# Attention's transfers on SP: each group waits for the landing of an earlier one, and k's two parts move as one run

## The chip, the cores and the metric

The kernel runs on one core of a Trainium2 chip. Its time is the device time of one execution in microseconds (us); three executions before the change took 1617.93, 1617.93 and 1624.52 us, so the median is 1617.93 us. Engines are named as in the profile: PE (TensorE matmul, PEld its weight load), DVE (VectorE), ACT (ScalarE), POOL (GpSimd), SP (SyncE, which here does nothing but issue transfers; the profile writes SPq). 16 DMA engines carry out the transfers that SP, ACT and POOL issue.

## The reference

One gated block on x of shape (16, 128, 1024) with a context of the same shape:

```python
x = x + tanh(g_xattn) * attention(layernorm(x), ctx)   # 8 heads of 16 channels, window of 16 positions
x = x + tanh(g_ffn)   * ffn(layernorm(x))              # weights int4-like integers, groups of 128

q = Wq x + bq ; k = Wk cond + bk ; v = Wv cond + bv    # pointwise over 128 channels
k, v are padded with 8 zeros on the left and 7 on the right of the 1024 positions
dots[b,h,t,w] = sum_d q[b,h,d,t] * k[b,h,d,t+w] / 4 ;  attn = softmax over w (16 places)
out = Wo (sum_w attn * v[.., t+w]) + bo
ffn = (silu(x Wgate) * (x Wup)) Wdown                  # 1024 -> 3584 -> 1024
```

k, q, v and the probabilities are held as a high and a low fp16 part whose sum carries the fp32 value; the products of both parts are summed.

## The kernel before

The span has two stages. The first 418 us or so are attention over the 16 batches, the rest is the feed-forward part, 14 passes over its hidden columns. The change touches attention only.

**One round of attention** (loop over `b`, 16 rounds) handles batch b in four steps (`s` = 0 to 3). A step's scores are 64 small matmuls (L1100) into two banks, the softmax runs on DVE (L896, L900), ACT (L679) and POOL (L546, L548), PE transposes the probabilities (L1111), ACT copies them (L684) and PE mixes them with v (64 matmuls, L1131). The projections of the batch after, b + 1, are set between those steps by `tasks_of`: k in step 0 (PE L1062, ACT L668 writes the high part, DVE L932 the low part), v in step 1 (PE L1058, ACT L662, DVE L928), q in step 2, and the output product of batch b - 1 in step 3. Every engine runs its own program in order; a semaphore wait at an instruction holds all that stands behind it on that engine.

**SP's part of a round** is a fixed list of issues, in this order: `keep_row(b - 2)` stores a finished batch to device memory (L423, 512 KB); `move_k(b + 1)` copies the two halves of k from `k_hl` into the staggered buffer `km` in 8 transfers of 64 KB, 16 partitions each (L394), SBUF to SBUF; `load_ctx(b + 2)` loads the next context (L382, 512 KB); `place_v(b + 1)` copies v from `vn_hl` into `vt` in two copies of 6 transfers each (L406, L408, L410), with 40, 8, 48, 48, 40 and 8 partitions (the last 8 and the first are the spill over the edge); `load_x(b + 2)` loads x (L376, 512 KB). In the kernel before, SP waits in this list only for engines: for k's low part (the wait in `move_k`, DVE L932), for v's low part, for buffers that the engines have read. It never waits for a transfer to land, except for `row_kept` of four batches ago and before the first weights of the second stage.

**Who waits for SP's transfers:** PE's scores of batch b + 1 for all 8 moves of k; PE's first mix of batch b + 1 for all 12 moves of v; PE's projections of k and v for the context; DVE's moments for x. Two waits go the other way round a buffer: ACT L668 may write k_hl only when the last batch's 8 moves have landed (`k_moved`), and ACT L662 may write `vn_hl` only when the last batch's 12 moves have landed (`v_placed`).

Of the kernel before, what the change touches and what calls it, by code (L numbers as in the profile page):

```python
# [4 lines left out]
def flamingo_layer(nc, x_in, ctx_in, g_xattn, g_ffn, WqT, bq, WkT, bk, WvT, bv, WoT, bo,  # L5
# [62 lines left out]
    with ctx:  # L68
# [26 lines left out]
        k_hl = sb("k_hl", [P, 2, T], fp16, att)  # L95
# [6 lines left out]
        km.append(sb("km1", [P, 2, HG, T + WIN], fp16, att))  # L102
# [40 lines left out]
        V_MOVES = 16 * 2 * (VW + 2)  # L143
# [5 lines left out]
        def slot_of(j):  # L149
# [28 lines left out]
            sem("zeroed"), sem("consts_made"), sem("masks_made"), sem("gates_ready"))  # L178
        km_zeroed = [sem("km0_zeroed"), sem("km1_zeroed")]
        bias_turned, bias_summed, bias_ready = sem("bias_turned"), sem("bias_summed"), sem("bias_ready")  # L180
        pad_hi, pad_lo, pad_placed, ones_placed = sem("pad_hi"), sem("pad_lo"), sem("pad_placed"), sem("ones_placed")
        x_loaded = [sem("even_x_loaded"), sem("odd_x_loaded")]
        ctx_loaded, k_moved, v_placed, row_kept = sem("ctx_loaded"), sem("k_moved"), sem("v_placed"), sem("row_kept")
# [185 lines left out]
        def _(sp):  # L369
            def load_x(b):  # L370
                if b >= 4:
                    sp.wait_ge(row_kept, 16 * (b - 3))
# [3 lines left out]
                sp.dma_start(rows[b % 4][:, :], x_in[b]).then_inc(x_loaded[b % 2], 16)  # L376

            def load_ctx(b):
# [3 lines left out]
                sp.dma_start(ct[:, :], ctx_in[b]).then_inc(ctx_loaded, 16)  # L382

            def move_k(b, halves=(0, 1)):

                sp.wait_ge(emptied_proj, low_done("k", b, 1))
                if b < 2:
# [8 lines left out]
            def place_v(b):  # L396
# [5 lines left out]
                for d in (0, KW):  # L402
                    for jj in range(VW):
                        lo, slot = QB * jj - PAD, jj * NV
                        a, z = max(lo, 0), min(lo + KW, P)
                        sp.dma_start(to[d + a - lo:d + z - lo, slot:slot + NV], vn_hl[a:z]).then_inc(v_placed, 16)  # L406
                        if lo < 0:
                            sp.dma_start(to[d:d - lo, slot + 1:slot + NV], vn_hl[P + lo:P, 0:NV - 1]).then_inc(v_placed, 16)  # L408
                        if lo + KW > P:
                            sp.dma_start(to[d + P - lo:d + KW, slot:slot + NV - 1], vn_hl[0:lo + KW - P, 1:NV])\  # L410
                              .then_inc(v_placed, 16)
# [891 lines left out]
```

## Time and profile before

| | |
|---|---|
| runs shown, median of 3 | 1617.93 us |
| profiled execution: its own time | 1623.17 us |
| profiled execution: span of the core | 1621.4 us |
| PE busy, of the span | 95% |
| DVE busy, of the span | 90% |
| granted TensorE clock, mean | 0.985 |
| SP's transfers (q1), share of 16 DMA engines, 60 to 380 us | 66.6% |

The profiled execution is 5.2 us above the median of the runs shown, and within what those runs span. A busy share is a mean over both stages. In attention the engines are less full than in the feed-forward part, and how SP spends a round is only seen in its list of issues in order of time: the start of an issue is where SP's wait ended, and its duration is what SP needs to hand it over, not what the transfer takes.

### The profile page before, as it was taken

The page shows a single profiled execution, that of the slowest core. Times are in us where ns is not written, and L with a number is a line of the kernel's source. Part 1 is how long each engine was busy: PE and PEld are TensorE (multiplying, and loading weights), DVE is VectorE, ACT ScalarE, POOL GpSimd, SP SyncE. Part 2 cuts the span into 40 slices and gives each one's busy share as a digit, 9 for nine tenths or more (in the row PEclk, how much of TensorE's full clock was granted, in tenths as well). Part 3 has the DMA queues.
Part 4 walks back from the last instruction along what each step waited for, and adds up shares of the span by engine and source line. Part 5 has one row for each costly group of instructions (what it writes and reads, how often), then busy time and mean ns, then how long its engine had stood idle before and what let it go on. Part 6 is the DMA issues. An engine that isn't in the chain of part 4 may idle for free.

```text
span 1621.4 us, 38499 instructions
## 1 busy us (share of the span) xinstructions
PE 1534.6 (95%) x15590; PEld 789.4 (49%) x15590; DVE 1454.5 (90%) x1425; ACT 1057.2 (65%) x1207; POOL 1262.2 (78%) x948
## 2 busy tenths in 40 slices
PE   6888898988799999999999999999999999999996
PEld 4565566665444444444444444444444444444444
DVE  4688788887798999999999999999999999999997
ACT  3677777877566666666666666666666666666652
POOL 3677677778455988888888888888888888888865
PEclk7899999999899999999999999999999999999999
DMA  4676766775353767666667676666666676666569
GB/s 126 171 155 140 172 145 148 173 159 138 118 143 98 152 154 155 152 151 152 147 153 156 156 155 151 149 153 152 152 155 156 144 156 156 153 152 151 116 182 324
DMA packets 192267, 250.16 MB, mean 154 GB/s; under 512 B 14446, under 2 KB 138030, under 8 KB 192074
## 3 DMA queue, kind: packets, MB, share of 16 engines
q1 hardware_dynamic: 167994, 164.26, 36.8%
q0 software_dynamic: 22752, 82.85, 29.1%
q8 instruction: 124, 2.03, 0.5%
q10 hardware_dynamic: 1344, 0.59, 0.2%
q14 instruction: 53, 0.43, 0.1%
HBM read 113.92 MB, written 16.78 MB: 81 GB/s over the span
## 4 chain that ended last, share of the span: by engine, by line
PE 86%; ACT 5%; issue 4%; POOL 2%; DVE 1%; DMA 1%; SPq 1%; ACTq 0%; DVEq 0%; POOLq 0%
PE bank L1193 69%; PE bank L1111 3%; PE bank L1100 2%; ACT pT L684 2%; PE bank L1066 2%; PE bank L1131 2%; PE bank L1073 2%; PE bank L1062 2%; PE bank L1058 1%; ACT vn_hl L662 1%; POOL oacc L628 1%; PE bank L1078 1%; PE bank L1090 1%; ACT pr L679 1%; ACT xn L692 1%
## 5 line engine op out<-in xcount | busy, mean ns | idle before, releaser
L988 DVE SCALAR_TENSOR_TENSOR acc<-bank,scale,acc 128x1024 f32<-128x1024 f32 x784 | 969.5, 1279 | 51.7 <-PE bank L1193 14.9
L1193 PE MATMUL bank<-xT,w_int 128*128 128x512 f16 x3584 | 847.8, 379 | 6.3 <-DVE xT L940 2.0
L628 POOL TENSOR_TENSOR oacc<-oacc,d_part 128x1024 f32<-128x1024 f32 x219 | 536.3, 2454 | 54.5 <-ACT d_part L832 49.0
L1193 PEld LDWEIGHTS bank<-xT,w_int 128*128 128x128 f16 x3584 | 350.3, 98 | 431.4 <-DVE xT L940 3.3
L832 ACT ACTIVATE d_part<-bank,scale 128x1024 f32<-128x1024 f32 x219 | 244.1, 1115 | 200.8 <-PE bank L1193 196.9
L1193 PE MATMUL bank<-h_hi,d_int 128*128 128x512 f16 x896 | 339.6, 379 | 2.1 <-ACT d_part L832 1.8
L1193 PE MATMUL bank<-h_lo,d_int 128*128 128x512 f16 x896 | 339.6, 379 | 0.0
L832 ACT ACTIVATE d_more<-bank,scale 128x1024 f32<-128x1024 f32 x158 | 176.2, 1115 | 154.4 <-PE bank L1193 154.4
L630 POOL DMA_DIRECT2D oacc<-d_more x158 | 149.9, 949 | 114.0 <-ACT d_more L832 107.8
L564 POOL TENSOR_TENSOR raw_z<-raw_w,raw_z 128x512 int32<-128x512 int32 x168 | 225.6, 1343 | 16.5 <-DMA raw_z<-in_L_ffn_gate_z_dram 8.3
L684 ACT ACTIVATE pT<-bank 96x1024 f16<-96x1024 f16 x128 | 130.2, 1017 | 38.3 <-PE bank L1111 37.9
L618 POOL TENSOR_TENSOR h_lo<-acc,h_hi 128x1024 f16<-128x1024 f32 x56 | 129.5, 2312 | 22.7 <-ACT h_hi L814 22.7
L1193 PEld LDWEIGHTS bank<-h_hi,d_int 128*128 128x128 f16 x896 | 87.7, 98 | 107.9 <-ACT d_part L832 2.0
L1193 PEld LDWEIGHTS bank<-h_lo,d_int 128*128 128x128 f16 x896 | 87.7, 98 | 104.3
L801 ACT ACTIVATE acc<-bank,scale 128x1024 f32<-128x1024 f32 x112 | 118.9, 1111 | 11.9 <-PE bank L1193 11.9
L546 POOL CAST p_hl<-pr 128x768 f16<-128x768 f32 x64 | 52.8, 824 | 73.8 <-ACT pr L679 68.4
L548 POOL TENSOR_TENSOR p_hl<-pr,p_hl 128x768 f16<-128x768 f32 x64 | 105.5, 1648 | 5.3
L1111 PE MATMUL bank<-ident,p_hl 128*128 128x128 f16 x1024 | 82.4, 224 | 8.4 <-issue 6.5
L896 DVE TENSOR_REDUCE rmax<-bank 128x16 f32<-128x768 f32 x64 | 61.1, 954 | 31.7 <-PE bank L1100 31.1
L995 DVE SCALAR_TENSOR_TENSOR acc<-acc 128x1024 f32<-128x1024 f32 x56 | 80.8, 1443 | 0.5
L806 ACT ACTIVATE acc<-acc 128x1024 f32<-128x1024 f32 x56 | 59.2, 1057 | 31.5 <-DVE acc L988 31.5
L1111 PEld LDWEIGHTS bank<-ident,p_hl 128*128 128x128 f16 x1024 | 64.8, 100 | 30.2 <-issue 23.9
(85 smaller groups left out, 1438.5 us busy)
## 6 DMA issues: line engine op xcount, KB each, us to landing
oacc<-d_more POOLq DMA_DIRECT2D x158, 512.0 KB, 5.0
raw_w<-in_L_ffn_gate_w_dram SPq DMA_DIRECT2D x56, 256.0 KB, 3.4
raw_z<-in_L_ffn_gate_z_dram SPq DMA_DIRECT2D x56, 256.0 KB, 4.2
raw_w<-in_L_ffn_up_w_dram SPq DMA_DIRECT2D x56, 256.0 KB, 3.4
raw_z<-in_L_ffn_up_z_dram SPq DMA_DIRECT2D x56, 256.0 KB, 4.0
raw_w<-in_L_ffn_down_w_dram SPq DMA_DIRECT2D x56, 256.0 KB, 3.1
raw_z<-in_L_ffn_down_z_dram SPq DMA_DIRECT2D x56, 256.0 KB, 3.7
vt<-vn_hl SPq DMA_DIRECT2D x64, 198.0 KB
```

The source lines that it names most:

```text
L548: nc.gpsimd.tensor_tensor(lo, src, hi, ALU.subtract).then_inc(p_lo, 1)
L564: nc.gpsimd.tensor_tensor(raw_z[:, slot], raw_w[:, slot], raw_z[:, slot], ALU.subtract)\
L618: nc.gpsimd.tensor_tensor(h_lo[:, q % 2, :], acc[:, q % 2, 0, :], h_hi[:, q % 2, :], ALU.subtract)\
L628: nc.gpsimd.tensor_tensor(into, into, d_part[:, (n - 1) % 2, :], ALU.add).then_inc(d_added, 1)
L630: nc.gpsimd.dma_start(into, d_more[:, (n - 1) % 2, :], accum_op=ALU.add).then_inc(landed(n)[0], 16)
L684: nc.scalar.activation(pT[0:2 * KW, n % 2, hg, :], turned[0:2 * KW, :], ACT.Copy).then_inc(pT_ready, 1)
L801: nc.scalar.activation(acc[:, q % 2, m, :], pair[u % 4][:, :, :].rearrange("p h r -> p (h r)"), ACT.Copy, scale=scale[:, par, i, m, 0:1]). ...
L832: nc.scalar.activation(part, pair[slot][:, :, :].rearrange("p h r -> p (h r)"), ACT.Copy, scale=scale[:, par, x // NCT % SC, 2, x % NCT:x ...
L988: nc.vector.scalar_tensor_tensor(out=into, in0=pair[u % 4][:, :, :].rearrange("p h r -> p (h r)"), scalar=scale[:, par, i, m, k:k + 1], in ...
L995: nc.vector.scalar_tensor_tensor(out=acc[:, q % 2, 0, :], in0=acc[:, q % 2, 1, :], scalar=1.0 / XS, in1=acc[:, q % 2, 0, :], op0=ALU.mult, ...
L1111: last = nc.tensor.transpose(turned[:, x * P:(x + 1) * P], p_hl[:, n % 2, at:at + P], ident16[:, :])
L1193: last = nc.tensor.matmul(dst[:, h, :], weights, rows_of(h, part), start=(part == 0), stop=(part == 1))
```

## The change

Four things change, all in attention.

1. k's high and low part lie in one row of 2056 numbers: 1024 high, 8 zeros, 1024 low (`K_LOW` = 1032), in `k_hl` and in `km`. A move then takes one run of 4,112 bytes from each of 16 partitions, where it took two of 2,048. The zeros serve as the right pad of the high part and the left pad of the low one; POOL sets them once (`gap_zeroed`).
2. The three 512 KB transfers of a round are issued as two halves of 64 partitions each, with a semaphore for each half.
3. Semaphores for k's moves are four in turn, for v's three in turn. SP issues a k move only when the one four before it has landed, and a v move only when the one three before has landed.
4. SP's list is reordered, and each group waits for the group before it (argument `room`): the context's halves for the last two moves of k, the first two v moves for the context's two halves, x's halves for the first copy of v, the second copy of v for x's halves, the stored rows for x's halves, and the next round's first two k moves for the stored row's halves. x is now loaded between the two copies of v.

```diff
-        k_hl = sb("k_hl", [P, 2, T], fp16, att)
+        K_LOW = T + PAD
+        k_hl = sb("k_hl", [P, K_LOW + T], fp16, att)
-        km = [sb("km0", [P, 2, HG, T + WIN], fp16, att)]
+        km = [sb("km0", [P, HG, K_LOW + T + WIN], fp16, att)]
...
+            PARTS = (slice(0, P // 2), slice(P // 2, P))
+            def load_ctx(b, room=()):
                 if b:
                     sp.wait_ge(projected, done("k", b - 1, 1))
                     sp.wait_ge(projected, done("v", b - 1, 1))
-                sp.dma_start(ct[:, :], ctx_in[b]).then_inc(ctx_loaded, 16)
+                for n, wait in enumerate(room or (None, None)):
+                    if wait:
+                        sp.wait_ge(*wait)
+                    sp.dma_start(ct[PARTS[n], :], ctx_in[b][PARTS[n]]).then_inc(ctx_loaded[n], 16)
...
                 for h in range(HG):
                     for hg in halves:
+                        i = 2 * h + hg
+                        if i < len(room):
+                            sp.wait_ge(*room[i])
+                        elif b and i > 3:
+                            sp.wait_ge(k_moved[i % 4], 32 * b + 16)
                         lo = GC * hg + HD * h
-                        sp.dma_start(km[b % 2][lo:lo + HD, :, h, PAD:PAD + T], k_hl[lo:lo + HD, :, :]).then_inc(k_moved, 16)
+                        sp.dma_start(km[b % 2][lo:lo + HD, h, PAD:PAD + K_LOW + T], k_hl[lo:lo + HD, :])                          .then_inc(k_moved[i % 4], 16)
...
+                        for dst, src in moves:
+                            if i - copy * (VW + 2) < len(room):
+                                sp.wait_ge(*room[i - copy * (VW + 2)])
+                            elif i > 2:
+                                sp.wait_ge(v_placed[i % 3], V_MOVES * b + 16 * (i // 3))
+                            sp.dma_start(dst, src).then_inc(v_placed[i % 3], 16)
+                            i += 1
...
                 if b >= 2:
-                    keep_row(b - 2)
+                    keep_row(b - 2, x_landed(b + 1) if b + 1 < B else ())
...
                 if b + 1 < B:
-                    move_k(b + 1)
+                    move_k(b + 1, room=kept(b - 2) if b >= 2 else ())
                 if b + 2 < B:
-                    load_ctx(b + 2)
+                    load_ctx(b + 2, [(turn, 32 * (b + 2)) for turn in k_moved[2:]])
                 if b + 1 < B:
-                    place_v(b + 1)
+                    place_v(b + 1, (0,), ctx_landed(b + 2) if b + 2 < B else ())
                 if b + 2 < B:
-                    load_x(b + 2)
+                    load_x(b + 2, [(turn, V_MOVES * (b + 1) + V_MOVES // 2) for turn in v_placed[1:]])
+                if b + 1 < B:
+                    place_v(b + 1, (1,), x_landed(b + 2) if b + 2 < B else ())
```

SP's program for one round of attention, before the change (`[waits ...]` are the semaphores that an issue waits for):

```order
L394 DMA km<-k_hl 16x2x1024 [waits scores_ready,emptied_proj]
L394 DMA km<-k_hl 16x2x1024 x7
L382 DMA ct<-in_ctx_dram 128x1024 [waits projected]
L406 DMA vt<-vn_hl 40x2112 [waits mix_ready,emptied_proj]
L408 DMA vt<-vn_hl 8x1848
L406 DMA vt<-vn_hl 48x2112 x2
L406 DMA vt<-vn_hl 40x2112
L410 DMA vt<-vn_hl 8x1848
```

Behind these stand the second copy of v, x's load and the stored row, the same way, without a wait for a landing. The same stretch of SP's program after the change, and what follows it to the next round's k:

```order
L419 DMA km<-k_hl 16x2056 [waits k_moved2]
L419 DMA km<-k_hl 16x2056 [waits k_moved3]
L400 DMA ct<-in_ctx_dram 64x1024 [waits k_moved2,projected]
L400 DMA ct<-in_ctx_dram 64x1024 [waits k_moved3]
L442 DMA vt<-vn_hl 40x2112 [waits ctx_half0_loaded,mix_ready,emptied_proj]
L442 DMA vt<-vn_hl 8x1848 [waits ctx_half1_loaded]
L442 DMA vt<-vn_hl 48x2112
L442 DMA vt<-vn_hl 48x2112 [waits v_placed0]
L442 DMA vt<-vn_hl 40x2112 [waits v_placed1]
L442 DMA vt<-vn_hl 8x1848 [waits v_placed2]
L391 DMA row<-in_x_dram 64x1024 [waits v_placed1,x_normed]
L391 DMA row<-in_x_dram 64x1024 [waits v_placed2]
```

```order
L442 DMA vt<-vn_hl 40x2112 [waits odd_x_half0_loaded,mix_ready,emptied_proj]
L442 DMA vt<-vn_hl 8x1848 [waits odd_x_half1_loaded]
L442 DMA vt<-vn_hl 48x2112 [waits v_placed2]
L442 DMA vt<-vn_hl 48x2112 [waits v_placed0]
L442 DMA vt<-vn_hl 40x2112 [waits v_placed1]
L442 DMA vt<-vn_hl 8x1848 [waits v_placed2]
L458 DMA rows_after_attention<-row 64x1024 [waits odd_x_half0_loaded,emptied_proj]
L458 DMA rows_after_attention<-row 64x1024 [waits odd_x_half1_loaded]
L419 DMA km<-k_hl 16x2056 [waits row_half0_kept,scores_ready,emptied_proj]
L419 DMA km<-k_hl 16x2056 [waits row_half1_kept]
```

x's load has moved ahead of the second copy of v, and nearly every issue now names a semaphore that a transfer raises when it lands. PE's program has the same matmuls in the same order; its waits for k, v and the context are now for 4, 3 and 2 semaphores where each was for one.

## Rows read from the trace of the kernel before

**Rows 1.** The page: the span
```profile
span 1621.4 us, 38499 instructions
```
**Rows 2.** SP in order of time, one round: start us, duration us, what
```profile
204.72 5.96 SPq L394 DMA_DIRECT2D km<-k_hl  x8
210.78 0.53 SPq L382 DMA_DIRECT2D ct<-in_ctx_dram  x1
211.40 0.82 SPq L406 DMA_DIRECT2D vt<-vn_hl  x1
...
220.82 0.55 SPq L376 DMA_DIRECT2D row<-in_x_dram  x1
221.42 0.42 SPq L423 DMA_DIRECT2D rows_after_attention<-row  x1
227.98 1.37 SPq L394 DMA_DIRECT2D km<-k_hl  x2
```
**Rows 3.** SP in order of time, issues of k's moves in four rounds
```profile
37.98 5.17 SPq L394 DMA_DIRECT2D km<-k_hl  x8
...
54.55 6.44 SPq L394 DMA_DIRECT2D km<-k_hl  x8
...
301.37 6.30 SPq L394 DMA_DIRECT2D km<-k_hl  x8
...
323.66 6.44 SPq L394 DMA_DIRECT2D km<-k_hl  x8
...
370.77 6.05 SPq L394 DMA_DIRECT2D km<-k_hl  x8
```
**Rows 4.** SP's waits, 60 to 380 us: total us, times, longest
```profile
SPq L394 <- DVE k_hl L932: 82.5, 13, 9.5
```
**Rows 5.** PE's waits, 60 to 380 us
```profile
PE bank L1058 <- issue: 9.0, 9, 1.5
PE bank L1131 <- issue: 8.8, 7, 2.4
PE bank L1111 <- issue: 6.5, 7, 1.7
```
**Rows 6.** PE in order of time: one break in three rounds
```profile
132.02 1.16 PE L1058 MATMUL bank<-wv,ct 128*128 128x128 f32 x8 [1.51 <-issue]
...
254.07 0.83 PE L1058 MATMUL bank<-wv,ct 128*128 128x128 f32 x6 [1.09 <-issue]
...
325.75 0.71 PE L1058 MATMUL bank<-wv,ct 128*128 128x128 f32 x4 [1.41 <-issue]
```
**Rows 7.** Transfers by queue, 60 to 380 us: packets, MB, share of 16 engines
```profile
q1 hardware_dynamic: 17570, 48.57, 66.6%
q8 instruction: 66, 1.08, 1.5%
```
**Rows 8.** Busy tenths of 16 DMA engines, 14 to 20 us, slices of 0.15 us
```profile
DMA  1000000000000039896779988966889842000000
```
**Rows 9.** SP in order of time: the k moves of that stretch
```profile
14.82 2.94 SPq L394 DMA_DIRECT2D km<-k_hl  x4
```
**Rows 10.** Issues: KB each, us to landing (60 to 67, 408 to 414 us)
```profile
ct<-in_ctx_dram SPq DMA_DIRECT2D x1, 512.0 KB, 3.4
...
rows_after_attention<-row SPq DMA_DIRECT2D x1, 512.0 KB, 2.6
```
**Rows 11.** The chain of waits, 0 to 60 us, and ACT's waits, 30 to 40 us
```profile
30.88 3.88 DMA vt<-vn_hl
...
ACT vn_hl L662 <- DMA vt<-vn_hl: 2.8, 1, 2.8
```
**Rows 12.** ACT in order of time: the first write of vn_hl in a round
```profile
229.67 0.62 ACT L662 ACTIVATE vn_hl<-bank 128x512 f16<-128x512 f32 x1 [1.65 <-PE bank L1058]
```
**Rows 13.** The transfers' queue, 207 to 210 us (k) and 214 to 219 us (v)
```profile
q1 hardware_dynamic: 214, 0.29, 64.3%
...
q1 hardware_dynamic: 243, 0.76, 87.0%
```

More of the change, by code:

```diff
@@ L401, in place_v @@
                 to = vt[b % 2]
-                for d in (0, KW):
+                for copy in copies:
+                    d, i = KW * copy, copy * (VW + 2)
                     for jj in range(VW):
@@ L419, in place_pads, with keep_row, x_landed, ctx_landed @@
                         sp.dma_start(vt[par][d + KW - PAD:d + KW, slot_of(NJ - 1)], v_pad[0:PAD]).then_inc(pad_placed, 16)
-            def keep_row(b):
+            def keep_row(b, room=()):
                 sp.wait_ge(emptied_proj, low_done("o", b, 1))
-                sp.dma_start(row_dram[b], rows[b % 4][:, :]).then_inc(row_kept, 16)
+                for n, wait in enumerate(room or (None, None)):
+                    if wait:
+                        sp.wait_ge(*wait)
+                    sp.dma_start(row_dram[b][PARTS[n]], rows[b % 4][PARTS[n], :]).then_inc(row_kept[n], 16)
+            def x_landed(b):
+                return [(half, 16 * (b // 2 + 1)) for half in x_loaded[b % 2]]
+            def ctx_landed(b):
+                return [(half, 16 * (b + 1)) for half in ctx_loaded]
+            def kept(b):
+                return [(half, 16 * (b + 1)) for half in row_kept]
             load_x(0)
@@ L660, in take_high @@
                     if n == 0 and b:
-                        act.wait_ge(v_placed, V_MOVES * b)
+                        for turn in v_placed:
+                            act.wait_ge(turn, V_MOVES * b)
                     nc.scalar.activation(vn_hl[:, 4 * n:4 * n + 4, :, 0:HD],
@@ L666, in take_high @@
                     if n == 0 and b:
-                        act.wait_ge(k_moved, 128 * b)
-                    nc.scalar.activation(k_hl[:, 0, n * HALF:(n + 1) * HALF], src, ACT.Identity, bias=bias[:, 1:2])\
+                        for turn in k_moved:
+                            act.wait_ge(turn, 32 * b)
+                    nc.scalar.activation(k_hl[:, n * HALF:(n + 1) * HALF], src, ACT.Identity, bias=bias[:, 1:2])\
                         .then_inc(high_taken, 1)
@@ L820, in scale_down @@
                     if n == 1:
-                        act.wait_ge(row_kept, 16 * B)
+                        for half in row_kept:
+                            act.wait_ge(half, 16 * B)
                         act.wait_ge(emptied_proj, len(low_place))
@@ L880, in moments_x @@
             def moments_x(b, halves=(0, 1)):
-                dve.wait_ge(x_loaded[b % 2], 16 * (b // 2 + 1))
+                for half in x_loaded[b % 2]:
+                    dve.wait_ge(half, 16 * (b // 2 + 1))
                 if b:
@@ L930, in take_low @@
                 elif kind == "k":
-                    hi, lo = (k_hl[:, part, n * HALF:(n + 1) * HALF] for part in range(2))
+                    hi, lo = (k_hl[:, K_LOW * part + n * HALF:K_LOW * part + (n + 1) * HALF] for part in range(2))
                     nc.vector.scalar_tensor_tensor(out=lo, in0=src, scalar=bias[:, 1:2], in1=hi,
@@ L1054, in project @@
                     if n == 0:
-                        pe.wait_ge(ctx_loaded, 16 * (b + 1))
+                        for load in ctx_loaded:
+                            pe.wait_ge(load, 16 * (b + 1))
                     for m in range(4):
@@ L1060, in project @@
                     if n == 0:
-                        pe.wait_ge(ctx_loaded, 16 * (b + 1))
+                        for load in ctx_loaded:
+                            pe.wait_ge(load, 16 * (b + 1))
                     last = nc.tensor.matmul(to[:, :], wk[:, :], ct[:, half],
```

62 lines of the change are left out of this document (39 added, 23 removed).

## The prediction, made before the changed kernel was run

> **What bounds the kernel now.** I read the page first, for the span of 1621.4 us [rows 1]: the attention stage is the only one that the change touches, and it is some 420 us of it. Then the program of SP in order of time, since all that changes are SP's issues. In the round shown, SP needs from 204.72 to 221.84 us for its list, 17.1 us, and the next k moves start at 227.98 (the table of the waits has DVE's low part of k as the reason) [rows 2, 4]. So SP has 82.5 us / 13 = 6.3 us of idle time in a round, and it follows the engines, not they it. The rounds themselves: k's moves of batch 2 start at 54.55, those of batch 15 at 370.77, 13 rounds in 316.2 us, 24.3 us each; the shortest takes 323.66 - 301.37 = 22.3 us [rows 3].
>
> Last the table of PE's waits. Between 60 and 380 us its three largest entries "issue" hold 9.0 + 8.8 + 6.5 = 24.3 us, 1.9 us a round [rows 5]. They are no wait for another engine: they fall in the middle of runs of equal matmuls, and the one in the projection of v stands with 8, 6 and 4 matmuls left in rounds at 132, 254 and 326 us [rows 6]. A break that slides by about one instruction pair over some rounds is tied to a position in the instruction stream, so it is PE waiting for its next block of instructions. Those blocks come through the same 16 DMA engines: 66 packets of 16 KB, each taking 1.5% of 16 x 320 us / 66 = 1.2 us of one engine, beside 66.6% of SP's transfers [rows 7]. Attention's engines are thus bound by their own chain (22 us a round or less) plus about 2 us of late instructions. Pacing can only give back of those 2 us; it pays in SP's list.
>
> **The one run of 4,112 bytes.** In a stretch of k moves 0.29 MB, or 141 packets of 2,048 bytes (the other 73 carry the landing signals), took 64.3% of 16 x 3 us, at most 0.22 us each; in a stretch of v, whose runs have 4,224 bytes, 0.76 MB or 180 packets took 87.0% of 16 x 5 us, 0.39 us each [rows 13]. Per move every DMA engine now has one packet of at most 0.39 us where it had two, together 0.44 us: 0.05 us earlier at best. If a run were as slow as v's and cut in two, it would cost 0.05 instead. The moves are paced by SP, 5.36 us from the first start to the eighth (5.96 less one issue of 0.60) [rows 2], so both ends are under 1 us over all rounds. I take 0. The cover is SP's issue time; the added zeros cost one memset at the start, beside x's load.
>
> **SP's list after the change.** Three landing times are needed, from the start of the issue.
> - A k move: the last of the four first ones starts at 14.82 + 2.94 - 0.60 = 17.16, and the DMA engines fall idle in slice 34, at 19.1 us [rows 8, 9]; with its signal, 2.3 us. It is the lower end for v as well.
> - A v move: between that 2.3 and the 3.88 us of the last one at the start, which had four or more in flight [rows 11]. With three in flight I take 2.9.
> - A half of 512 KB: the whole lands in 3.4 us as a load and 2.6 us as a store when little else is on its way [rows 10]. The whole gives every DMA engine 8 packets of 4,096 bytes; half of them, at 0.16 us or more each, saves 0.6 to 0.7. I take 2.7 and 2.1.
>
> Now the list, with 0 at the first k move of a round. Moves 7 and 8 start at 4.6 and 5.4 and land at 6.9 and 7.7; the fifth to eighth do not wait, for 4 x 0.77 is more than 2.3. The context's halves, which wait for them, start at 6.9 and 7.7 and land at 9.6 and 10.4. The first two moves of v wait for these. With 0.75 a move and three in flight, the six start at 9.6, 10.4, 11.15, 12.5, 13.3, 14.05, and the last two land at 16.2 and 16.95. x's halves wait for those and land at 18.9 and 19.65. The second copy of v starts then: 18.9, 19.65, 20.4, 21.8, 22.55, 23.3, handed over at 24.0. The stored halves start at 24.0 and 24.4 and land at 26.1 and 26.5, and the next k move waits for the first. That is a closed chain of 26.1 us. I add 0.6: a transfer lies on all 16 DMA engines and lands with the slowest, five blocks of instructions of 1.2 us fall into a round, and in a chain that waits for eight landings some of them meet one. So 26.7 us, of which 9 or so are waits for landings; SP had 6.3 us to hide them in. SP becomes the bound, and its idle time goes.
>
> Who waits for it: the first write of vn_hl on ACT, which needs all 12 v moves of the batch before. It stands at 229.67, 1.7 us behind the start of k's moves at 227.98 [rows 12, 2]; SP's last v move of the batch before was handed over before 220.82 [rows 2], so it had some 5 us of air. In the new chain the last v move lands at 26.2, about when the next k moves start, and ACT's exponentials and PE's mixes queue behind that write. That the coupling is real is seen at the start, where ACT waited 2.8 us for v's moves [rows 11]. Behind it PE waits with its scores, so the 2 us of late instructions lie inside a wait that is longer: they come sooner, and nothing is won.
>
> **The sum.** Batch 0's v is also moved three at a time: 12 moves in 4 x 2.9 = 11.6 us where the 12 of a round take 220.82 - 211.40 = 9.4 [rows 2], so the first full group of k starts at 37.98 + 2.2 = 40.2 [rows 3]. There is no stored row in the next two lists: 24.0 + 0.6 later, at 64.8, the second starts, where it started at 54.55: +10. Then 13 rounds at 26.7 - 24.3 = +2.4: +31. Together +41 us. The rest of the program is as it was. Against the profiled execution that is 1623.2 + 41 = 1664; the median of the runs shown lies 5 us lower, so I forecast **1659 us**, 2.5% slower.
>
> The Trainium skill, "DMA: Bandwidth & Descriptors", section "Rules for kernel authors", speaks against the halves: two transfers to disjoint partition halves serialize, use one with 128 partitions. In this case they go one behind the other anyway, since SP issues them 0.8 us apart; by the rule the second half would land up to 0.7 us later in each of three groups, and the sum would be 1659 + 13 x 2 = 1685. No row of before shows two halves alone.
>
> **Bounds of the unknown.** With v landing in 2.3, halves in 2.4 and 1.9, and nothing for instructions, the chain shrinks by 3 x 0.6 (v) + 2 x 0.3 + 0.2 + 0.6 to 23.5; that is 0.8 under today's round. With v at 3.88 it grows by 3 x 1.0, to 29.7, that is +5.4 a round and +17 at the start, +87 in all; but that value was taken with more in flight, so I let it weigh half: 28.2, +3.9 a round and +13 at the start, +64, which is 1682.
>
> **The rivals.**
> - *It does what it is built for* (faster). SP's chain stays under the round, and blocks of instructions come sooner. For it: the lower bound of the chain is 23.5, and the breaks cost 24.3 us in the table [rows 5]. Against: it needs every landing at its lower end, and after a break the next one comes with an idle queue as well. If half the breaks go, -12 us, and with 4 us lost at the start 1610.
> - *The chain just fits* (no change). 24.3 a round, the start loses 8 us, half the breaks give back 8: 1618.
> - *The halves and landings cost more under one another* (1682 or more), as in the upper bound above: the same mechanism, the size off.
> - *The run does not act*: a packet of 4,112 bytes is cut or slower. Worth under 1 us in any case, as above.
>
> The Trainium skill, "DMA: Bandwidth & Descriptors", section "Queues, rings and completion order", says that a DMA engine goes round its queues packet by packet. By that rule a block of instructions waits for one packet of SP's queue, 0.2 to 0.39 us, however many stand behind; pacing could give back 18 breaks x 0.3 = 5 us at most, and the first rival would end at 1617. The rows of the queue do not show when a block was asked for, so the trace leaves it open.
>
> **Chances.** SP-bound and slower as worked out: 0.70; more than that, over 1690 as towards the full upper bound of 1705: 0.08; SP-bound by little, 1627 to 1633: 0.07; the chain fits: 0.07; faster: 0.08. A measurement of this kernel can tell about 0.5%, 8 us, from no change. Slower by more than that 0.85, within it 0.07, faster 0.08. The range that holds the time 8 times in 10 goes from the chain at 25.1 us (13 x 0.8 + 9, less some us of breaks) to a little over the half-weighted upper bound: 1630 to 1690.
>
> **What would show it.** Right: k's moves in SP's list start 26 to 27 us apart from batch 3 on; the waits of SP name transfers, or nothing, and no longer DVE's low part of k; ACT's first write of vn_hl waits several us a round for v's moves; DMA share in attention falls by a tenth; the second stage keeps its length of 1,200 us. The step on landings is wrong if the groups follow each other in under 2.4 us; the step on the coupling is wrong if SP's chain takes 26 us and the engines still do not wait. The forecast fails if rounds stay at 24.3 us or less.

## The result, and the profile after

The changed kernel takes 1741.91 us (median of 4 runs, 1734.5 to 1742.07), the kernel before on the same chip 1621.22 us (4 runs): ratio 1.0711, 95% interval 1.0674 to 1.0747. It is slower, as forecast, but by 121 us and not by 41; 1659 us was the forecast, 1690 the end of its range.

Page of the changed kernel: the span, and the chain that ended last by engine.

```profile
span 1740.0 us, 38674 instructions
PE 71%; DMA 18%; SPq 3%; issue 3%; POOL 2%; DVE 2%; ACT 2%; ACTq 0%; DVEq 0%; POOLq 0%
```

SP in order of time in the changed kernel (start us, duration us, what): the first group of v, four groups of k, and below them one whole round, which answers to [rows 2, 3].

```profile
24.64 14.44 SPq L442 DMA_DIRECT2D vt<-vn_hl  x12
...
44.53 4.96 SPq L419 DMA_DIRECT2D km<-k_hl  x8
...
72.57 5.31 SPq L419 DMA_DIRECT2D km<-k_hl  x8
...
230.49 1.15 SPq L458 DMA_DIRECT2D rows_after_attention<-row  x2
233.61 5.78 SPq L419 DMA_DIRECT2D km<-k_hl  x8
240.56 1.16 SPq L400 DMA_DIRECT2D ct<-in_ctx_dram  x2
244.27 5.72 SPq L442 DMA_DIRECT2D vt<-vn_hl  x6
252.41 1.73 SPq L391 DMA_DIRECT2D row<-in_x_dram  x2
255.74 6.05 SPq L442 DMA_DIRECT2D vt<-vn_hl  x6
261.89 1.15 SPq L458 DMA_DIRECT2D rows_after_attention<-row  x2
...
488.24 5.96 SPq L419 DMA_DIRECT2D km<-k_hl  x8
```

From batch 2's k moves to batch 15's are 488.24 - 72.57 = 415.7 us, 13 rounds of 32.0 us, where there were 24.3 [rows 3] and 26.7 were forecast. Batch 15's k moves start 488.24 - 370.77 = 117.5 us later than before [rows 3], and the profiled execution is 1741.77 - 1623.17 = 118.6 us longer: all of the loss has been made by then, and the rest of the program is as it was.

The waits of the changed kernel, 60 to 500 us (total us, times, longest), SP's first, which answer to [rows 4], then the largest of ACT, PE and DVE.

```profile
SPq L442 <- DMA vt<-vn_hl: 36.3, 54, 2.9
SPq L439 <- DMA row<-in_x_dram: 34.2, 14, 3.6
SPq L439 <- DMA ct<-in_ctx_dram: 34.1, 13, 3.1
SPq L390 <- DMA vt<-vn_hl: 28.4, 14, 3.4
SPq L415 <- DMA rows_after_attention<-row: 24.7, 13, 2.0
SPq L399 <- DMA km<-k_hl: 15.4, 13, 1.9
...
ACT vn_hl L713 <- DMA vt<-vn_hl: 150.3, 14, 13.6
...
PE bank L1191 <- ACT pT L736: 115.1, 15, 11.5
...
DVE vn_hl L984 <- ACT vn_hl L713: 61.2, 28, 4.6
```

SP no longer waits for DVE's low part of k; its six largest rows are transfers. They hold 173.1 us, 12.6 us a round of 32.0. ACT stands 150.3 / 14 = 10.7 us a round before its first write of vn_hl, and PE's mixes and DVE's low part of v stand behind it. The chain of work that ended last, taken from 60 to 380 us and by line, has the same finding from the other end: its transfers and SP's own lines hold 79%. In the kernel before the largest share was a matmul's, and no transfer was among the first twelve.

```profile
by line: DMA vt<-vn_hl 38.7%; DMA row<-in_x_dram 13.1%; DMA ct<-in_ctx_dram 8.6%; DMA km<-k_hl 6.2%; SPq L442 5.9%; PE bank L1124 4.2%; DMA rows_after_attention<-row 4.1%; PE bank L1170 3.1%; PE bank L1159 2.7%; issue 2.5%; SPq L419 2.1%; A
```

Issues of the changed kernel, 60 to 500 us: KB each, median us from issue to landing.

```profile
km<-k_hl SPq DMA_DIRECT2D x112, 64.2 KB, 2.4
row<-in_x_dram SPq DMA_DIRECT2D x28, 256.0 KB, 4.0
ct<-in_ctx_dram SPq DMA_DIRECT2D x26, 256.0 KB, 4.2
rows_after_attention<-row SPq DMA_DIRECT2D x26, 256.0 KB, 3.1
```

A k move lands as forecast (2.3). A half of 512 KB does not: 4.0 to 4.2 us as a load, where 2.7 was taken, and 3.1 as a store, where 2.1 was. That is more than the 3.4 and 2.6 of the whole [rows 10]. These are medians over both halves. Read issue by issue, the first half of a load lands in 3.7 us (context) and 3.6 (x), the second in 4.3 and 4.2; the stored halves in 3.0 and 3.2.

### The profile page after: what moved, and what is told of

Read it like the earlier page. It is cut to its first block, busy times and chain, and to the rows that moved or that the text cites. A ratio compares the mean times of both kernels' runs of the same rounds, so it can differ in the third digit from the quotient of the medians.

```text
span 1740.0 us, 38674 instructions
## 1 busy us (share of the span) xinstructions
PE 1551.7 (89%) x15590; PEld 799.6 (46%) x15590; DVE 1457.6 (84%) x1425; ACT 1057.6 (61%) x1207; POOL 1262.0 (73%) x949
## 4 chain that ended last, share of the span: by engine, by line
PE 71%; DMA 18%; SPq 3%; issue 3%; POOL 2%; DVE 2%; ACT 2%; ACTq 0%; DVEq 0%; POOLq 0%
PE bank L1253 65%; DMA vt<-vn_hl 10%; DMA row<-in_x_dram 4%; DMA ct<-in_ctx_dram 2%; SPq L442 1%; DMA km<-k_hl 1%; PE bank L1170 1%; PE bank L1124 1%; PE bank L1159 1%; PE bank L1191 1%; POOL oacc L678 1%; ACT pT L736 1%; DMA rows_after_attention<-row 1%; SPq L419 1%; ACT vn_hl L713 0%
## 5 line engine op out<-in xcount | busy, mean ns | idle before, releaser
L614 POOL TENSOR_TENSOR raw_z<-raw_w,raw_z 128x512 int32<-128x512 int32 x168 | 225.5, 1343 | 20.2 <-DMA raw_z<-in_L_ffn_gate_z_dram 12.6
L680 POOL DMA_DIRECT2D oacc<-d_more x158 | 150.3, 951 | 114.1 <-ACT d_more L887 107.8
L1191 PE MATMUL bank<-vt,pT 96*32 96x33 f16 x4096 | 44.0, 185 | 120.2 <-ACT pT L736 118.7
L713 ACT ACTIVATE vn_hl<-bank 128x512 f16<-128x512 f32 x32 | 19.8, 621 | 160.3 <-DMA vt<-vn_hl 158.7
L1191 PEld LDWEIGHTS bank<-vt,pT 96*32 96x32 f16 x4096 | 37.5, 96 | 143.4 <-ACT pT L736 134.4
L929 DVE BATCH_NORM_STATS2 stats<-row 128x6 f32<-128x512 f32 x64 | 43.5, 684 | 69.6 <-issue 49.4
L1170 PE MATMUL bank<-ident,p_hl 128*128 128x128 f16 x1024 | 88.2, 235 | 3.1 <-ACT pT L736 1.7
```

The source lines that it names most:

```text
L614: nc.gpsimd.tensor_tensor(raw_z[:, slot], raw_w[:, slot], raw_z[:, slot], ALU.subtract)\
L680: nc.gpsimd.dma_start(into, d_more[:, (n - 1) % 2, :], accum_op=ALU.add).then_inc(landed(n)[0], 16)
L1170: last = nc.tensor.transpose(turned[:, x * P:(x + 1) * P], p_hl[:, n % 2, at:at + P], ident16[:, :])
L1191: last = nc.tensor.matmul(mixed[jg][c, VS * h:VS * h + V1], pT[0:2 * KW, n % 2, h // HG, at:at + QB], vt[b % 2][0:2 * KW, slot_of(JQ * s + ...
```

## The experiments

In all of them a round is the distance of the k moves of batches 2 and 15 in SP's list, divided by 13, of the profiled execution; ratios are to the kernel before, run beside them.

**1. The run of 4,112 bytes alone, in the kernel before.**

```diff
-    sp.dma_start(km[b % 2][lo:lo + HD, :, h, PAD:PAD + T], k_hl[lo:lo + HD, :, :])
+    sp.dma_start(km[b % 2][lo:lo + HD, h, PAD:PAD + K_LOW + T], k_hl[lo:lo + HD, :])
```

> The kernel before with k's two parts moved as one run of 4,112 bytes and nothing else. Theory (SP's list of waits for landings makes the whole loss): the run is worth nothing, 1618 to 1624 us, ratio within 0.3% of 1, rounds of 24.3 us. Rival (the long run itself is slow, since its packets took 0.42 us in the changed kernel): landings of k come late, rounds over 25 us, 1640 or more.

Measured: ratio 1.0015 [0.9993, 1.0037], rounds of (376.39 - 55.20) / 13 = 24.7 us, and SP waits for DVE's low part of k as before (86.7 us, 13 times). The run is worth nothing by itself. What the halves and the new place of x's load are worth without the waits is in experiment 10: together they are a small part of the loss.

**2. The changed kernel without the waits between groups.**

```diff
-    keep_row(b - 2, x_landed(b + 1) if b + 1 < B else ())
+    keep_row(b - 2)
-    load_ctx(b + 2, [(turn, 32 * (b + 2)) for turn in k_moved[2:]])
+    load_ctx(b + 2)
     (and so for k, both copies of v, and x)
```

> The changed kernel without the waits between groups (no room arguments); the halves, the order, four k moves and three v moves in flight stay. Theory: SP's list is 5.8 (k) + 14.4 (12 v moves, three in flight, as at the start of the changed kernel's list) + 3 x 1.15 (halves) = 23.7 us a round, just under the engines' 24.3, so nearly all of the loss goes: 1620 to 1635 us. Rival (the limit of moves in flight costs the most): rounds stay over 28 us, 1690 or more.

**3. The changed kernel without the turns within k's and v's groups.**

```diff
-    elif b and i > 3:
-        sp.wait_ge(k_moved[i % 4], 32 * b + 16)
...
-    elif i > 2:
-        sp.wait_ge(v_placed[i % 3], V_MOVES * b + 16 * (i // 3))
```

> The changed kernel without the limits of moves in flight (waits on the turns of k_moved and v_placed inside a group); the waits between groups stay. Theory: each copy of v is handed over in 4.6 instead of 5.6 us and lands a little later, so a round takes 29 to 30.5 us instead of 32.0 and the time is 1700 to 1720 us. Rival (the limit in flight makes the loss): close to 1640.

Measured: without the waits between groups 1652.01 us, 1.0175 [1.0146, 1.0204], rounds of (397.82 - 66.86) / 13 = 25.5; without the turns 1718.81 us, 1.0583 [1.0545, 1.0621], rounds of (467.64 - 65.66) / 13 = 30.9. So the six waits between groups make 32.0 - 25.5 = 6.5 us of the 7.7 us that a round has grown by, and the turns 1.1 while those stand. The first of the two ended above what was expected, 1620 to 1635 us. SP's and ACT's waits in it, 60 to 500 us, say why:

```profile
SPq L442 <- DMA vt<-vn_hl: 75.0, 32, 3.7
...
ACT vn_hl L713 <- DMA vt<-vn_hl: 53.3, 10, 8.7
```

The turns of v alone still make SP late for ACT in 10 rounds. The first kernel of experiment 10 is this one without the turns: 1.0077 for 1.0175, so they cost about 1% here.

**4. The changed kernel with whole transfers** of 512 KB for x, context and stored rows; all waits stand, those of a half and of its sibling now ahead of the one transfer.

```diff
-    PARTS = (slice(0, P // 2), slice(P // 2, P))
+    PARTS = (slice(0, P),)
...
-    for n, wait in enumerate(room or (None, None)):
-        if wait:
-            sp.wait_ge(*wait)
+    for wait in room:
+        sp.wait_ge(*wait)
+    for n in range(1):
         sp.dma_start(ct[PARTS[n], :], ctx_in[b][PARTS[n]]).then_inc(ctx_loaded[n], 16)
... (and so for x and the stored rows)
```

> The changed kernel with each 512 KB transfer whole again, its one issue waiting for all that its two halves waited for, all other waits kept. What the prediction took (a half lands 0.7 us before a whole one, plus 0.8 us until the second half is issued): +2 us a round, 1765 us or more. Theory now (a half of two in flight lands in 4.1 us, a whole one alone in 3.4): equal to the changed kernel or better, rounds of 30.5 to 32 us, 1722 to 1742.

**5. The changed kernel with its halves cut by columns:** 128 partitions of 2,048 bytes, not 64 of 4,096.

```diff
-    PARTS = (slice(0, P // 2), slice(P // 2, P))
+    PARTS = (slice(0, T // 2), slice(T // 2, T))
...
-    sp.dma_start(ct[PARTS[n], :], ctx_in[b][PARTS[n]]).then_inc(ctx_loaded[n], 16)
+    sp.dma_start(ct[:, PARTS[n]], ctx_in[b][:, PARTS[n]]).then_inc(ctx_loaded[n], 16)
... (and so for x and the stored rows)
```

> The changed kernel with the halves cut by columns (128 partitions, 2,048 bytes each) instead of by partitions (64 partitions, 4,096 bytes). Theory: what a half costs is the fixed part of a transfer plus its neighbour's packets on the same 16 DMA engines, so the halves land in 3.9 to 4.2 us as before and the time is 1735 to 1745 us. Rival (64 partitions reach fewer ports, so a half has a whole one's data time): halves land in 3.0 to 3.4 us, two loads and a store a round save 2 to 2.5 us, 1705 to 1715.

Measured: whole transfers 1739.09 us, 1.0708 [1.0671, 1.0746], rounds of (488.63 - 71.42) / 13 = 32.1; column halves 1708.92 us, 1.0512 [1.047, 1.0553], rounds of (454.37 - 67.66) / 13 = 29.7. The landings, first with whole transfers, then with column halves (60 to 500 us, columns as above):

```profile
row<-in_x_dram SPq DMA_DIRECT2D x14, 512.0 KB, 3.5
ct<-in_ctx_dram SPq DMA_DIRECT2D x13, 512.0 KB, 3.6
rows_after_attention<-row SPq DMA_DIRECT2D x13, 512.0 KB, 2.9
```

```profile
rows_after_attention<-row SPq DMA_DIRECT2D x30, 256.0 KB, 2.6
row<-in_x_dram SPq DMA_DIRECT2D x27, 256.0 KB, 3.1
ct<-in_ctx_dram SPq DMA_DIRECT2D x26, 256.0 KB, 2.9
```

By these medians a half on 64 partitions lands 0.2 to 0.6 us later than the whole (4.0, 4.2, 3.1 against 3.5, 3.6, 2.9), and a half on 128 partitions 0.3 to 0.7 earlier. Read issue by issue, and in the order context, x, stored row:

```
                               first half         second half
halves of 64 partitions        3.7, 3.6, 3.0      4.3, 4.2, 3.2
halves by columns              2.7, 2.9, 2.3      3.1, 3.7, 2.6
whole                          3.6, 3.5, 2.9
```

So the first half on 64 partitions is no earlier than a whole, and the second of a load is 0.6 us later still. The packets show a part of it (60 to 500 us, read one by one): the 5,120 packets of 4,096 bytes have a median of 0.25 us each in the changed kernel and of 0.16 with whole transfers; the packets of 2,048 bytes of the column halves have 0.08. It is not all of it: four packets of 0.25 us are 1.0 us, and the eight of a whole 1.3. The columns take 2.3 us off a round. The size that the forecast took, 0.6 to 0.7 us less for half the bytes, is right for column halves and wrong for the halves that the change makes. Of the two theories put down before this run the rival held, in the landings (3.0 to 3.4 us expected) and in the time (1705 to 1715); the cause that it names, ports, is in no row.

The Trainium skill, "DMA: Bandwidth & Descriptors", section "Rules for kernel authors", says to use one transfer of 128 partitions rather than two to disjoint halves, because the two serialize. For the second half of a load the trace agrees (4.3 and 4.2 us for the first's 3.7 and 3.6). That reason does not cover that the first half lands no earlier than a whole.

**6. Both edits of 3 and 5 together** (no diff of its own).

> The changed kernel without the turns within k's and v's groups, and with its halves cut by columns (128 partitions of 2,048 bytes) and not by partitions; the waits between groups all stand. Apart, the first edit took 1.1 us off a round and some 21 us off the whole, the second 2.3 us and some 31 us. Theory (SP's list is a sum of landings, so both add): rounds of 28.4 to 28.9 us, 1680 to 1696 us, ratio 1.034 to 1.044. Were the forecast's small landings all that was wrong with it, 26.7 us a round and 1659 us. Rival (one saving hides the other, or another engine becomes the bound): over 1700.

Measured: 1684.64 us, 1.0361 [1.0322, 1.04], rounds of (436.93 - 63.62) / 13 = 28.7. Landings 3.0 (context), 2.9 (x), 3.1 (stored). The savings add, 1.1 and 2.3 apart and 3.3 together, as they should where a round is the sum of the landings in SP's list.

**7. Is anything but SP's list a bound?** A second copy of pT on ACT, some 5 us a round, put into the changed kernel and, for comparison, into the kernel before.

```diff
     act.wait_ge(probs_turned, 2 * n + hg + 1)
+    if hg:
+        nc.scalar.activation(pT[0:2 * KW, n % 2, hg, :], turned[0:2 * KW, :], ACT.Copy).then_inc(twice, 1)
+        act.wait_ge(twice, n + 1)
     nc.scalar.activation(...)
```

> The changed kernel with the second copy of pT in each step done twice on ACT (4 more activations of 1.02 us a round, about 5 us of ACT's time). Theory: SP's list is the only bound of a round, ACT idles 10 us a round at the write of vn_hl, so the time is the changed kernel's within 10 us. Rival (the engines' chain shares the path): 30 us or more on top.

> The kernel before with the same doubled copy, for comparison. Theory: here the engines' chain, in which the copy of pT stands, is the bound, and the time grows by 16 rounds x 2 to 5 us = 32 to 80 us, to 1650 to 1700. Rival (ACT has the time): under 10 us.

Measured: the changed kernel 1739.4 us, 1.0699 [1.0658, 1.074], no different from 1.0711 without the added work; the kernel before 1659.92 us, 1.021 [1.0169, 1.0252], 34 us more than the 1625.98 us run beside it, rounds of (404.98 - 57.49) / 13 = 26.7 for 24.3. ACT's waits in the changed kernel with the added work, 60 to 500 us:

```profile
ACT vn_hl L714 <- DMA vt<-vn_hl: 93.1, 14, 9.2
```

It had been 150.3: the added work took the place of waiting, and cost nothing. In the kernel before, the engines' chain is the bound and pays for it: SP's wait for DVE's low part of k grows there from 6.3 to 107.5 / 13 = 8.3 us a round. Work was added to ACT alone; PE and DVE were not tried.

**8. From which point does a wait cost?** The kernel before, first with one of the change's waits (the store waits for x's landing), then with two (v's first move waits for the context as well, from batch 1 on).

```diff
-    def keep_row(b):
+    def keep_row(b, x_of=None):
         sp.wait_ge(emptied_proj, low_done("o", b, 1))
+        if x_of is not None:
+            sp.wait_ge(x_loaded[x_of % 2], 16 * (x_of // 2 + 1))
...
     (the second kernel: also in place_v)
+        if b and b + 1 < B:
+            sp.wait_ge(ctx_loaded, 16 * (b + 2))
```

> The kernel before with one wait added: SP stores a finished row only when the x load before it has landed. Theory: a wait for a landing is free while SP has idle time in its list; this one costs 4 us of the 6 us at the list's end, and two 512 KB transfers no longer lie on top of each other when PE fetches its instructions, so the breaks in PE shrink by a part: 1606 to 1620 us, ratio 0.992 to 1.0. Rival (any wait for a landing lengthens the round): 1630 or more.

> The kernel before with two of the changed kernel's six waits: the store waits for x's landing (as in the run with that wait alone, which cost nothing), and the first v move of a batch row waits for the landing of the context load just issued. Theory (SP's list is a chain whose length adds up, and it costs only what it exceeds the engines' round by): with the first wait alone SP still stood 1.9 us a round for k's low part, so that much air is left; a context load of 512 KB lands 3.4 us after its issue, and SP issues only one other thing (0.6 us) in that time, so the list grows by 2.8 to 3.0 us, 1.0 to 1.2 us over the air, times 13 rounds = 13 to 16 us: 1634 to 1642 us, ratio 1.006 to 1.012, rounds of 25.6 to 26.0 us, and SP's wait for k's low part at or near 0. Rival (a wait is paid for in full wherever it stands): +39 us, 1660. Rival (only the half loads cost, whole loads with a wait never do): 1620 to 1626.

Measured: one wait 1622.14 us, 0.9972 [0.9948, 0.9995]; two 1629.52 us, 1.0029 [1.0007, 1.0052]. SP's waits, 60 to 500 us, with one wait and with two:

```profile
SPq L424 <- DMA row<-in_x_dram: 63.8, 13, 6.3
SPq L394 <- DVE k_hl L934: 24.6, 13, 3.8
```

```profile
SPq L426 <- DMA row<-in_x_dram: 51.7, 13, 4.7
SPq L402 <- DMA ct<-in_ctx_dram: 43.0, 13, 5.0
...
SPq L394 <- DVE k_hl L936: 3.0, 3, 1.9
```

Read the last row of each beside [rows 4]: 82.5 us of waiting for DVE fall to 24.6 and then to 3.0, while the waits for transfers grow to 63.8 and to 94.7. The first wait was paid from SP's idle time. The second used it up, and the kernel is slower by 0.3%, less than the 0.6 to 1.2% expected and only just clear of nothing. The rounds, (373.14 - 52.41) / 13 = 24.7 us with one wait and (382.06 - 57.52) / 13 = 25.0 with two, are of one execution each and too coarse for such a step: 24.7 stands beside a time that has not grown. Waits of this kind were free while the row of the engine's waiting still held 1.9 us a round and began to cost when it was nearly empty.

The expectation of the first kernel had a second part that did not come: with the wait the stored row lands in 3.4 us and not in 6.5, yet "issue", the time in which an engine waited for nothing that the profile shows, has 10.6% of the chain of work from 60 to 380 us, and 10.2% before. Setting x's load and the stored row apart did not by itself take anything from PE's breaks.

**9. v's moves one at a time, in the kernel before.**

```diff
+    if i:
+        sp.wait_ge(v_placed, V_MOVES * b + 16 * i)
     sp.dma_start(dst, src).then_inc(v_placed, 16)
```

> The kernel before with v's twelve moves of a batch row one at a time, each waiting for the landing of the one before; nothing else. It measures the landing of a v move when nothing else of v is under way. Theory A (a move of v takes 3.7 us however few are in flight, as with three): SP's group takes 11 x 3.7 + 0.6 = 41 us, rounds of about 49 us, some 1950 us. Theory B (it is 2.9 or less when few are in flight, as the forecast took for three): the group 32 us or less, rounds of 40 us or less, 1830 us or less.

Measured: 1916.86 us, 1.1796 [1.177, 1.1823], rounds of (640.52 - 101.64) / 13 = 41.5. SP in order of time, two stretches of v, and its waits from 60 to 500 us:

```profile
199.68 27.84 SPq L415 DMA_DIRECT2D vt<-vn_hl  x10
...
236.30 22.58 SPq L415 DMA_DIRECT2D vt<-vn_hl  x9
```

```profile
SPq L415 <- DMA vt<-vn_hl: 258.5, 116, 4.0
```

From issue to issue (27.84 - 0.6) / 9 = 3.0 and (22.58 - 0.6) / 8 = 2.7 us: a v move that is alone lands in 2.9 us on average. By size, and as medians of all rounds from 60 to 500 us, the next issue stands 2.9 to 3.1 us behind a move of 40 or 48 partitions and 2.3 behind one of 8. With three in flight, in the round of the changed kernel above, the fifth move has landed 252.41 - 244.27 = 8.1 us after the first was issued; 0.75 + 2 landings = 8.1 gives 3.7 us. So the landing grows with what is in flight, as theory B has it, and the 2.9 us of the forecast belong to one move in flight and not to three. The group, 11 x 2.9 + 0.6 = 32.5 us, is theory B's; its 1830 us, 13 x (40 - 24.3) = 204 us on top of the kernel before, fell short for one thing by the start: batch 2's k moves stand at 101.64 for 54.55 us, 47 us later.

**10. What is left of the change without its pacing waits, and part by part.** First the changed kernel without any pacing wait: what is left is the run of 4,112 bytes, the halves, and x's load between the two copies of v. Then, in the kernel before, the place of x's load alone (the diff), and place and run; last the first kernel again with column halves.

```diff
     if b + 1 < B:
-        place_v(b + 1)
+        place_v(b + 1, (0,))
     if b + 2 < B:
         load_x(b + 2)
+    if b + 1 < B:
+        place_v(b + 1, (KW,))
```

> The changed kernel with all the waits that pace it taken out, between groups and within them: what is left of the change is the run of 4,112 bytes, the halves of 64 partitions, and x's load put between the two copies of v. With the waits between groups out alone, 1652 us were measured, SP's wait for v's turns being 67 us in 26 waits. Theory (three v moves in flight are what that version paid for): without them SP's list is shorter than the engines' round again, rounds of 24.3 to 24.9 us, 1620 to 1632 us, ratio 0.998 to 1.005, and SP waits for k's low part of ACT or DVE again. Rival (halves of 64 partitions cost in themselves, since they crowd the moves): 1640 to 1655, rounds over 25.2, with x or the context late for DVE or PE.

> The kernel before with one thing of the change, the place of x's load: between the two copies of v and not behind both; whole transfers, no new wait. The changed kernel without any of its pacing waits (run, halves, this place) was 0.8% slower than before, with rounds of 24.9 us and SP waiting 32.4 us in 12 waits at x's load for ACT to have read the row before it. Theory (the place does it: x's load asks for its row some 5 us earlier, before ACT has given it up, and the second copy of v stands behind that wait): SP waits for ACT at x's load, 2 to 3 us a round, ratio 1.004 to 1.010, rounds of 24.6 to 25.0 us. Rival (the halves of 64 partitions cost it, by a later landing): ratio 0.998 to 1.002, and the waits at x's load are as short as here or have no one behind them.

> The kernel before with x's load between the two copies of v and k's two parts as one run of 4,112 bytes; whole transfers, no new wait. Theory (the run is worth nothing, as alone: 1.0015): the order's gain stays, 0.993 to 0.998, and the halves carry all of the 1.4% between this and the changed kernel without its waits. Rival (the run costs with this order): 1.000 or more.

> The changed kernel without its pacing waits, its halves cut by columns (128 partitions of 2,048 bytes). Cut by partitions the same kernel took 1.0077 of the kernel before, and whole transfers at the same place in the order 0.9941. Theory (the shape of 64 partitions costs, by loading some of the DMA engines more and so holding up the blocks of instructions: PE's waits 'issue' in the scores rose to 20.4 us in 18): ratio 0.993 to 0.999, those waits back at some 10 us. Rival (two transfers where there was one cost it, by SP's three further issues a round and by more packets): 1.004 to 1.009.

Measured:

```
                               ratio   95% interval      round, us                    K of batch 2
place, run, 64-part. halves    1.0077  1.0049 to 1.0106  (383.81 - 59.52)/13 = 24.9   59.52
place alone                    0.9941  0.9923 to 0.9959  (361.64 - 54.63)/13 = 23.6   54.63
place and run                  0.9943  0.9923 to 0.9962  (366.07 - 53.70)/13 = 24.0   53.70
place, run, column halves      0.9928  0.9908 to 0.9949  (364.57 - 57.97)/13 = 23.6   57.97
```

("K of batch 2": start of its k moves, us.) Each ratio is to the kernel before run beside it. Two expectations fell. The halves of 64 partitions cost 1.3% (1.0077 against 0.9943) though the issue of no transfer waits for them, and the place of x's load, which was blamed for it, is a gain of 0.6%: the kernel with the place alone is faster than the kernel before and than the changed one. Of the 7.1% that the changed kernel loses the pacing waits thus make 1.0711 - 1.0077, 6.3 of the 7.1. SP does wait 29.5 us in 12 waits at x's load for ACT, as was expected, and it costs nothing, for SP still waits for DVE behind it. SP's waits with the place alone, 60 to 500 us:

```profile
SPq L394 <- DVE k_hl L934: 47.4, 13, 6.0
SPq L375 <- ACT xr L703: 29.5, 12, 3.9
```

Where the gain comes from is not shown, only pointed to. x's loads and stored rows land in 4.1 and 4.3 us (60 to 380 us), where they took 5.9 and 6.5 while issued 0.6 us apart behind both copies of v, and the chain's share "issue" of 320 us falls from 10.2% to 7.6%, 8 us for 9.6 gained. The loss and the gain of the halves agree with that: "issue" has 11.3% with the halves of 64 partitions and 7.7% with columns. But with place and run it has 9.5% at the same 0.994, and PE's waits "issue" at the scores, which should have fallen from 20.4 us to some 10 with the columns, fell to 15.0 (60 to 380 us).

**11. The two edits that were not slower, together:** the place of x's load and the store behind x's landing.

> The kernel before with x's load between the two copies of v (0.9941 alone) and the store waiting for x's landing (0.9972 alone). Theory (the wait falls into SP's idle time, which the earlier load of x leaves as it was, since x has landed by the time of the store): the store waits under 1 us, nothing changes against the order alone, ratio 0.992 to 0.996. Rival (each spreads the transfers, so both gains add): 0.989 to 0.992.

Measured: 1614.8 us, 0.9934 [0.9916, 0.9952]; SP waits for x's landing 3.1 us in 2 waits. The wait adds nothing where the place has already set the transfers apart. The best time of the study is the place's, 1614 to 1615 us.

## Why the forecast was right in kind and wrong in size

- *What bounds the kernel, and the closed chain.* Right. SP had 6.3 us of idle time a round, the new list is longer than the engines' round, and SP's waits name transfers in all but 4.4 us. Experiment 7 shows that ACT's work is not a bound any more, 6 that the list's parts add, 8 about where its air ends.
- *Who waits.* Right: ACT's first write of vn_hl, 10.7 us a round, and PE and DVE behind it.
- *The run is worth 0.* Right: 1.0015 [0.9993, 1.0037].
- *A k move lands in 2.3.* Right: 2.4 us, and the context's first half is issued 240.56 - 233.61 = 6.95 us after the first k move, where 6.9 was worked out.
- *The landings of the halves and of v.* This step failed, and it is the whole miss. In the round shown:

```
                          forecast   measured                      more
context half to v         2.7        244.27 - 240.56 = 3.7         1.0
first copy of v to x      6.6        252.41 - 244.27 = 8.1         1.5
x half to second copy     2.7        255.74 - 252.41 = 3.3         0.6
second copy of v          5.1        261.89 - 255.74 = 6.15        1.05
stored half to next k     2.1        265.03 - 261.89 = 3.1         1.0
```

Together 5.2 us. The round shown takes 265.03 - 233.61 = 31.4 us, 5.3 more than the list's 26.1; the mean round takes 32.0, 5.3 more than the forecast's 26.7. Half of it are the half transfers: the term "a half of 512 KB: 2.7 and 2.1" took packets off the whole's time and left the time of a packet at 0.16 us, where 0.25 was measured for halves of 64 partitions: the first half lands no earlier than a whole. The other half are v's moves: "with three in flight I take 2.9" was the time of one alone, 3.7 was measured. The row of 3.88 us [rows 11] stood near the truth, and letting it weigh half, because more were in flight there, was the wrong choice. With it in full and the halves of the table, the working gives 26.7 + 3.0 + 1.0 + 0.6 + 1.0 = 32.3 us a round.
- *The start.* Batch 0's twelve v moves take 14.4 us where 4 x 2.9 = 11.6 was reckoned; k's first full group starts at 44.5 and not 40.2, the second at 72.6 and not 64.8. That is 7.8 us more, with 13 x 5.3 = 69 for the rounds 77 us, of the 118.6 - 41 = 78 us missed.
- *The rival from the page's rule*, halves one behind the other for 1685 us, pointed the right way and was 57 us short. Its 0.7 us for the second half of a load was measured as 0.6; it holds nothing for v, and nothing for a first half that is as late as a whole.
- *The rival that pacing makes instructions come sooner.* The chain's share "issue" falls from 10.2% to 2.5%, hidden behind a wait five times as long, as forecast. Whether some such time is to be had by spreading transfers stays open: the place of x's load wins 0.6%, but its cause is not shown. The 5 us that the prediction allows this rival at most are not sound: [rows 5] have 9 + 7 + 7 = 23 breaks and not 18, and the packet after which a DMA engine changes its queue was taken to be one packet of the profile, which no row shows.
- *The signs.* The waits of SP and of ACT came as described, the rounds came out at 32.0 us and not at 26 to 27. DMA share in attention fell from 0.68 to 0.51, by a quarter and not by a tenth, which goes with the longer rounds (24.3 / 32.0 = 0.76). The second stage kept its length, as forecast.
- *The range.* All five terms of the table missed in the same direction. The upper end of v alone already gave 1705, and even that is 37 us short, for the halves had stayed at 2.7 and 2.1 in it. Letting one end weigh half and leaving the other at its point made the range too short.

## What to carry to other kernels

In this kernel a wait for a landing was free on the engine that issues the transfers while that engine still waited for the other engines, and was paid for once that waiting was used up. So add up the landings of the new list from issue to landing, and compare with the round. Take a landing from a row of the same shape with as many in flight; a smaller transfer need not be a faster one. Where a tile has to be moved in halves, try half the columns on all partitions: half the partitions landed no sooner than the whole tile here. Before pacing transfers by waits, try another place in the list.

## What the runs showed that was not expected

- In the paced kernels 256 KB on 64 partitions land in 4.0 to 4.2 us as loads (3.6 to 3.7 the first half), 512 KB on 128 in 3.5 to 3.6, 256 KB on 128 in 2.9 to 3.1; and without any wait on them the first shape makes the kernel 1.3% slower than whole transfers. It shows in the packets, 0.25 us for 4,096 bytes instead of 0.16; through what, the runs do not tell, and which DMA engines carry a packet is in no row.
- A v move (28.9 to 198 KB in the table of issues) lands on average 2.9 us after its issue when alone, 3.7 us with three in flight.
- PE's granted clock is lower in the paced stage. Busy time of the attention stage before and after (us, then PE and the others busy with counts, granted clock, DMA share, GB/s), and the second stage after:

```profile
60.00:380.00 320.00, 280.72 (x8328) 197.57 (x8325) 264.93 (x425) 247.94 (x333) 230.63 (x265) 0.99 0.68 156
```

```profile
60.00:500.00 440.00, 308.43 (x8560) 216.07 (x8558) 273.93 (x434) 255.01 (x340) 237.68 (x273) 0.86 0.51 119
600.00:1700.00 1100.00, 1099.73 (x5095) 498.26 (x5094) 1050.88 (x847) 708.85 (x751) 925.66 (x572) 1.00 0.68 151
```

PE's granted clock is 0.99 before and 0.86 after, a mean over stretches at 2.4 GHz and at 1.2. In the round shown PE does nothing from about 258.5 us until its mixes start at 265.12, and three stretches read:

```profile
259.00:263.00 4.00, 0.00 (x0) 0.00 (x0) 1.57 (x3) 0.00 (x0) 1.05 (x3) 1.00 0.60 151
264.00:270.00 6.00, 4.82 (x140) 3.23 (x141) 3.94 (x7) 5.20 (x8) 3.04 (x3) 0.50 0.49 100
271.00:275.00 4.00, 3.91 (x148) 2.76 (x146) 2.71 (x7) 4.00 (x7) 2.29 (x5) 1.00 0.45 104
```

Over the whole stage a matmul takes 308.43 / 8560 = 36.0 ns on average, for 280.72 / 8328 = 33.7. That lies inside the round that SP sets. Experiment 7 shows that 5 us more of ACT's work a round are not paid for there; for PE's slower matmuls it is argued from that and not measured.
